# Two-layer sandwich on one core: the sums of squares of all four tiles by one selection product, and a new order of all calls

## The reference

```python
def attn(x, Wq1, Wq2, Wk1, Wk2, Wv, Wo, norm_w):
    q = silu(x @ Wq1 @ Wq2)
    f = sigmoid(x @ Wk1 @ Wk2)
    v = x @ Wv
    a = exp(log_sigmoid(f))
    k = 1.0 - a
    h = scan(h = a * h + k * v)                      # along the tokens
    out = q * h
    out = out * rsqrt(mean(out * out, axis=-1) + 1e-6) * norm_w
    return out @ Wo

def ffn(x, W1, B1, W2, B2, G, Bt):
    for i in range(6):
        x = gelu(x @ W1[i].T + B1[i]) @ W2[i].T + B2[i] + x
        if i < 5:
            x = layernorm(x) * G[i] + Bt[i]
    return x

x = x + layernorm(attn(layernorm(x), ...))
x = x + layernorm(ffn(layernorm(x), ...))
```

## Time and profile before

| | us |
|---|---|
| median of 3 runs | 627.94 (627.71 to 628.29) |
| the profiled execution, its own time | 629.86 |
| its span, first to last instruction | 628.0 |
| TensorE busy | 619.8 (99%) |
| VectorE busy | 470.1 (75%) |
| ScalarE busy | 407.9 (65%) |
| GpSimd busy | 250.4 (40%) |
| TensorE's granted clock over the span | 0.998 |

### The profile page before, as it was taken

How to read it: one execution, slowest core, us unless ns; L and a number is a source line. 1 busy time by engine, 2 the same in 40 slices (tenths; PEclk the granted TensorE clock), 3 DMA queues, 4 the chain that set the end, 5 groups by cost and what they waited for, 6 DMA issues and landing times.

```text
span 628.0 us, 8878 instructions
## 1 busy us (share of the span) xinstructions
PE 619.8 (99%) x2893; PEld 516.4 (82%) x2893; DVE 470.1 (75%) x820; ACT 407.9 (65%) x688; POOL 250.4 (40%) x232
## 2 busy tenths in 40 slices
...
GB/s 285 62 47 0 1 2 0 4 17 88 38 38 40 10 64 6 5 36 38 42 33 5 40 39 2 72 7 4 37 40 38 36 5 6 5 4 76 119 106 103
DMA packets 56877, 25.13 MB, mean 40 GB/s; under 512 B 47360, under 2 KB 52864, under 8 KB 56832
## 3 DMA queue, kind: packets, MB, share of 16 engines
...
...
## 4 chain that ended last, share of the span: by engine, by line
PE 92%; DVE 3%; issue 2%; ACT 2%; POOL 1%; POOLq 0%; DVEq 0%; ACTq 0%
PE BK L169 47%; PE BK L351 38%; PE BK L301 3%; PE BK L175 1%; PE BK L366 1%; PE BK L198 1%; DVE OL L534 1%; PE BK L242 0%; POOL X L1188 0%; ACT R L835 0%; PE BK L262 0%; PE BK L253 0%; PE BK L254 0%; PE BK L232 0%; ACT R L849 0%
## 5 line engine op out<-in xcount | busy, mean ns | idle before, releaser
L945 ACT ACTIVATE HH<-BK,B 128x512 fp32r<-128x512 f32 x192 | 132.1, 688 | 140.5 <-PE BK L169 136.2
L563 DVE TENSOR_TENSOR HL<-BK,HH 128x512 fp32r<-128x512 f32 x192 | 130.7, 683 | 83.3 <-ACT BK L951 82.8
L169 PE MATMUL BK<-XH,WL 128*128 128x512 f32 x416 | 162.5, 391 | 0.7 <-DVE HL L563 0.7
L169 PE MATMUL BK<-XL,WH 128*128 128x512 f32 x416 | 162.1, 390 | 0.0
L169 PE MATMUL BK<-XH,WH 128*128 128x512 f32 x416 | 162.0, 389 | 0.0
L351 PE MATMUL BK<-HH,WL 128*128 128x512 f32 x368 | 143.7, 390 | 0.0
L351 PE MATMUL BK<-HH,WH 128*128 128x512 f32 x368 | 143.2, 389 | 0.0
L351 PE MATMUL BK<-HL,WH 128*128 128x512 f32 x368 | 143.2, 389 | 0.0
L951 ACT ACTIVATE BK<-BK,B 128x512 f32<-128x512 f32 x192 | 125.8, 655 | 0.0
L169 PEld LDWEIGHTS BK<-XH,WL 128*128 128x128 f32 x416 | 78.1, 188 | 17.3 <-DVE HL L563 1.1
L169 PEld LDWEIGHTS BK<-XH,WH 128*128 128x128 f32 x416 | 78.1, 188 | 16.5
(11 more groups left out here) (149 smaller groups left out, 793.8 us busy)
## 6 DMA issues: line engine op xcount, KB each, us to landing
...
G<-sums SPq DMA_DIRECT2D x160, 8.0 KB, 1.8
...
sums<-P SPq DMA_DIRECT2D x40, 8.0 KB, 1.4
...
```

What stands on the lines that cost most here:

```text
L169: r = eng.matmul(dst, s, m, start=i == 0, stop=i == len(todo) - 1)
L563: eng.tensor_tensor(HL[:, g % HR, :], bank["mm1", n, j][:, :], HH[:, g % HR, :].bitcast(f32), ALU.subtract).then_inc(S["hlo"], 1)
L945: eng.activation(HH[:, g % HR, :], bank["mm1", n, j][:, :], ACT.Gelu, bias=B1[:, 8 * (n // 4) + j:8 * (n // 4) + j + 1]).then_inc(S["ghi"], 1)
```

## The change

It takes away the path with the vector of ones for tiles 0 and 1: all four tiles now run `sq_turn`, `sq_part`, one selection matmul and four `ms`. `sel()` moves from the middle of VectorE's list to its start, ahead of `ulo(0, 0)`. The written-out lists of all engines are in a new order: TensorE's up to `mm2(3, 4)`, VectorE's up to tile n = 5 and from n = 21 on, ScalarE's up to n = 4 and from n = 22 on, GpSimd's up to n = 1 and from n = 20 on, and SyncE's after its loop. No other call is added or taken away, and the loops are as before. The diff, cut:

```diff
             def rms(t, b):
                 claim(b)
-                if t < 2:
-                    pe.wait_ge(S["ssum"], 3 * t + 3)
-                    pe.wait_ge(S["one"], 1)
-                    for c in range(4):
-                        r = eng.matmul(BK[b][:, c:c + 1], SB[:, 0, c * 128:(c + 1) * 128], ONE[:, :],
-                                       start=(c == 0), stop=True, skip_group_check=True)
-                else:
-                    pe.wait_ge(S["sq_part"], t - 1)
-                    pe.wait_ge(S["sel"], 1)
-                    r = eng.matmul(BK[b][:, 0:16], SEL[:, :], PR[:, :], start=True, stop=True)
+                pe.wait_ge(S["sq_part"], t + 1)
+                pe.wait_ge(S["sel"], 1)
+                r = eng.matmul(BK[b][:, 0:16], SEL[:, :], PR[:, :], start=True, stop=True)
                 r.then_inc(S["rms"], 1)
...
-            zq(0, 2, 0); zk(0, 0, 1); v(0, 0, 2); zk(0, 1, 3); v(0, 1, 4); zk(0, 2, 5); zq(0, 3, 1); v(0, 2, 0)
-            zk(0, 3, 3); v(0, 3, 2); proj(0, 0); turn1(1, 0, 5); turn1(1, 1, 3); proj(0, 1); up(1, 0, 1); up(1, 1, 4)
-            u(1, 0); u(1, 1); proj(0, 2); zq(1, 0, 0); zq(1, 1, 5); zk(1, 0, 3); v(1, 0, 1); zq(1, 2, 2); zq(1, 3, 4)
-            rms(0, 0); zk(1, 1, 3); proj(0, 3); v(1, 1, 5); zk(1, 2, 2); v(1, 2, 3); zk(1, 3, 4); turn1(2, 0, 0)
+            zq(0, 2, 0); zk(0, 0, 1); v(0, 0, 2); zk(0, 1, 3); v(0, 1, 4); zk(0, 2, 5); v(0, 2, 0); zk(0, 3, 3)
+            zq(0, 3, 1); v(0, 3, 2); turn1(1, 0, 5); proj(0, 0); turn1(1, 1, 3); proj(0, 1); up(1, 0, 1); u(1, 0)
+            up(1, 1, 4); u(1, 1); proj(0, 2); zq(1, 0, 0); zq(1, 1, 5); zk(1, 0, 3); v(1, 0, 1); zq(1, 2, 2)
+            zq(1, 3, 4); zk(1, 1, 3); proj(0, 3); v(1, 1, 5); zk(1, 2, 2); rms(0, 0); v(1, 2, 3); turn1(2, 0, 0)
+            turn1(2, 1, 1); zk(1, 3, 4); v(1, 3, 2); up(2, 0, 0); u(2, 0); up(2, 1, 5); u(2, 1); proj(1, 0)
...
-            mm1(1, 6, 3); proj(3, 3); mm2(1, 3); rms(3, 2); mm1(1, 7, 0); mm2(1, 4); mm2(1, 5); mm2(1, 6)
-            mm1(2, 0, 1); mm2(1, 7); mm1(2, 1, 2); mm1(2, 2, 3); mm2(2, 0); mm1(2, 3, 0); turn3(3, 0, 1)
-            turn3(3, 1, 2); mm2(2, 1); mm1(2, 4, 3); mm2(2, 2); mm1(2, 5, 1); mm2(2, 3); mm1(2, 6, 2); mm2(2, 4)
-            mm1(2, 7, 0); mm1(3, 0, 3); mm2(2, 5); mm1(3, 1, 1); mm2(2, 6); mm1(3, 2, 2); mm2(2, 7); mm1(3, 3, 0)
-            mm2(3, 0); mm1(3, 4, 3); mm2(3, 1); mm1(3, 5, 1); mm2(3, 2); mm1(3, 6, 2); mm2(3, 3); mm1(3, 7, 0)
+            turn3(2, 1, 0); mm1(1, 6, 3); proj(3, 2); proj(3, 3); mm1(1, 7, 0); rms(3, 2); mm2(1, 4); mm2(1, 5)
+            mm1(2, 0, 1); mm1(2, 1, 2); mm2(1, 6); mm1(2, 2, 3); mm1(2, 3, 0); mm2(1, 7); mm2(2, 0); mm2(2, 1)
+            turn3(3, 0, 1); turn3(3, 1, 2); mm2(2, 2); mm1(2, 4, 3); mm1(2, 5, 1); mm1(2, 6, 2); mm2(2, 3); mm2(2, 4)
+            mm1(2, 7, 0); mm1(3, 0, 3); mm1(3, 1, 1); mm2(2, 5); mm2(2, 6); mm2(2, 7); mm1(3, 2, 2); mm2(3, 0)
+            mm1(3, 3, 0); mm1(3, 4, 3); mm1(3, 5, 1); mm2(3, 1); mm2(3, 2); mm1(3, 6, 2); mm2(3, 3); mm1(3, 7, 0)
...
-            def ms(t, h=None):
+            def ms(t, h):
                 ve.wait_ge(S["rms"], t + 1)
-                if h is None:
-                    eng.tensor_scalar(MS[:, t, :], bank["rms", t][:, 0:4], *to_ms(t)).then_inc(S["ms"], 1)
-                    return
...
             def sq_part(t):
-                ve.wait_ge(S["sq_turn"], t - 1)
-                if t > 2:
+                ve.wait_ge(S["sq_turn"], t + 1)
+                if t:
                     ve.wait_ge(S["rms"], t)
...
-            f_nm(3); wq1_lo(); first_xlo(0); first_xlo(1); wk1_lo(); ulo(0, 0); ulo(0, 1); q(0, 0); q(0, 1); q(0, 2)
+            f_nm(3); wq1_lo(); first_xlo(0); first_xlo(1); wk1_lo(); sel(); ulo(0, 0); ulo(0, 1); l1_st(1, 0)
...
-            ulo(1, 0); o(0, 3); ulo(1, 1); l1_st(2, 2); olo(0, 3); q(1, 0); l1_st(2, 3); q(1, 1); l1_mv(2, 0)
-            l1_mv(2, 1); l1_mv(2, 2); l1_mv(2, 3); l1_st(3, 0); l1_st(3, 1); l1_st(3, 2); l1_st(3, 3); kv(1, 0)
-            q(1, 2); q(1, 3); ms(0); scan(1, 0); l2_st(0, 0); l2_st(0, 1); l2_st(0, 2); o(1, 0); l2_st(0, 3)
+            xlo1(1, 1); l1_st(2, 2); kv(0, 3); olo(0, 2); scan(0, 3); ulo(1, 0); o(0, 3); ulo(1, 1); l1_mv(2, 2)
+            l1_st(2, 3); l1_st(3, 0); l1_st(3, 1); l1_st(3, 2); l1_mv(2, 3); olo(0, 3); q(1, 0); kv(1, 0); q(1, 1)
+            scan(1, 0); q(1, 2); o(1, 0); sq_turn(0); l2_st(0, 0); sq_part(0); l2_mv(0, 0); l2_st(0, 1); l2_st(0, 2)
+            l2_st(0, 3); ms(0, 0); ms(0, 1); l2_mv(0, 1); ms(0, 2); ms(0, 3); l2_mv(0, 2); l2_mv(0, 3); kv(1, 1)
+            q(1, 3); scan(1, 1); xlo1(2, 0); xlo1(2, 1); o(1, 1); l3_st(0, 0); kv(1, 2); l3_st(0, 1); olo(1, 0)
...
+            hlo(2, 0); hlo(2, 1); y(1, 0); hlo(2, 2); tr2(0); red2(0); hlo(2, 3); y(1, 1); xlo3(3, 0); xlo3(3, 1)
+            tr1(1); tot2(0); vae(0); red1(1); hlo(2, 4); rsb(0); hlo(2, 5); hlo(2, 6); hlo(2, 7); nn(0, 0); tot1(1)
+            mub(1); ctr(1, 0); hlo(3, 0); y(2, 0); nn(0, 1); ctr(1, 1); hlo(3, 1); y(2, 1); hlo(3, 2); tr2(1); red2(1)
+            hlo(3, 3); xlo(0, 0); tr1(2); xlo(0, 1); hlo(3, 4); red1(2); hlo(3, 5); hlo(3, 6); tot2(1); hlo(3, 7)
```

ScalarE's and GpSimd's new lists around the same place:

```diff
+            l2_nm(3, 1); ghi(2, 0); gf(2, 0); l2_nm(3, 2); l2_nm(3, 3); ghi(2, 1); sqr(0, 0); ghi(2, 2); gf(2, 1)
+            gf(2, 2); l3_nm(3, 0); sqr(0, 1); l3_nm(3, 1); l3_nm(3, 2); l3_nm(3, 3); ghi(2, 3); gf(2, 3); xn(3, 0)
+            xn(3, 1); xhi3(3, 0); xhi3(3, 1); ghi(2, 4); gf(2, 4); ghi(2, 5); ghi(2, 6); wp_hi(5); gf(2, 5); gf(2, 6)
+            ghi(2, 7); wp_hi(6); ghi(3, 0); gf(2, 7); gf(3, 0); sqr(1, 0); ghi(3, 1); wp_hi(7); ghi(3, 2); gf(3, 1)
+            sqr(1, 1); wp_hi(8); ghi(3, 3); gf(3, 2); ghi(3, 4); xhi(0, 0); gf(3, 3); xhi(0, 1); ghi(3, 5); gf(3, 4)
...
-            sum1(0); l3_ve(2); l3_ng(2); l3_rs(2); l3_nb(2); ssum(3, 2); ssum(3, 3); sum2(0); l2_ve(3); l2_ng(3)
-            l2_rs(3); l2_nb(3); x1(3, 0); x1(3, 1); x1(3, 2); x1(3, 3); l3_ng(3); l3_ve(3); l3_rs(3); wp_lo(5, 0)
-            l3_nb(3); wp_lo(5, 1); rsd(0); sum1(1); wp_lo(6, 0); wp_lo(6, 1); wp_lo(7, 0); wp_lo(7, 1); wp_lo(8, 0)
-            sum2(1); wp_lo(8, 1)
+            x1(3, 0); x1(3, 1); x1(3, 2); x1(3, 3); l3_ve(3); l3_ng(3); l3_rs(3); l3_nb(3); sum2(0); sum1(1); rsd(0)
+            wp_lo(5, 0); wp_lo(5, 1); wp_lo(6, 0); wp_lo(6, 1); wp_lo(7, 0); wp_lo(7, 1); wp_lo(8, 0); wp_lo(8, 1)
+            sum2(1)
...
```

More of the change, by code:

```diff
@@ L721, in _ @@
-            sq_part(3); ctr(0, 1); hlo(1, 5); l2_st(3, 0); l2_st(3, 1); l2_st(3, 2); l2_st(3, 3); ms(3, 0); ms(3, 1)
-            ms(3, 2); ms(3, 3); l2_mv(3, 0); l2_mv(3, 1); l2_mv(3, 2); tr2(0); l2_mv(3, 3); hlo(1, 6); red2(0)
-            hlo(1, 7); l3_st(3, 0); l3_mv(3, 0); l3_st(3, 1); l3_mv(3, 1); l3_st(3, 2); l3_mv(3, 2); l3_st(3, 3)
-            l3_mv(3, 3); hlo(2, 0); y(1, 0); tot2(0); y(1, 1); vae(0); hlo(2, 1); hlo(2, 2); rsb(0); xlo3(3, 0)
-            nn(0, 0); xlo3(3, 1); hlo(2, 3); tr1(1); nn(0, 1); red1(1); hlo(2, 4); xlo(0, 0); xlo(0, 1); hlo(2, 5)
```

204 lines of the change are left out of this document (99 added, 105 removed).

## The result

| kernel | median, us | runs | ratio to before, 95% interval |
|---|---|---|---|
| before | 627.88 (627.71 to 628.29) | 4 | 1 |
| after | 643.28 (642.82 to 644.37) | 4 | 1.0247 (1.0229 to 1.0264) |

A forecast was written before the change was run, and what follows sets the result against it. The prediction took TensorE, busy for 619.8 of 628.0 us, to set the end. Its terms, from -1.3 for the instructions to +2.2 for the largest stall, summed to +1.2 on 627.94, so 629.1 us, range 625.9 to 631.6.

The forecast's parts named there:

- 46 to 118: From 46 to 118 us: the same calls in slightly other places, VectorE idle for a fifth; 0 (0 to +1.0).
- The main step: 150 to 170 us: `put1(1)` held behind `ldp(7)`, so TensorE waits about 2 us behind `hlo(3, 0)`.
- The start: Up to `zq(0, 0)`: first products come earlier, `sel` takes part of that back; -0.2 us (-0.4 to +0.3).
- 20 to 33: 20 to 33 us: GpSimd's later squares may spare `olo(0, 2)`, its `l1_nb(1)` calls delay `wo_lo`; -0.3 us (-1.0 to +0.3).
- 33 to 46: 33 to 46 us: full VectorE delays `q(1, 3)`, stalling TensorE before `zk(1, 3)`; +1.0 us (0 to +2.0).
- 118 to 150: 118 to 150 us: less waiting at tile 3's `proj`, -0.3; `turn3(3, 0)` earlier as `wp_lo(5, 0)` moved, -0.7 us.
- 150 to 170: 150 to 170 us: a 23.6 us chain to `mm2(3, 0)` against TensorE's 21.3; stall +2.2 us (0 to +3.2).
- Behind it: After `hlo(3, 0)`: 10.5 us of calls up to `hlo(3, 3)` against 9.5 of matmuls; +1.0 us (0 to +1.5).
- The end: Kernel's end: the wait at 595 us stays, `z_ct(3, 0)` stands one call earlier; -0.2 us.
- B: Tile 1's chain, 150 to 170 us and behind, ends under its cover, both stalls fall away: 625.9 us, chance 0.24.
- D: Whole kernel: the new order changes nothing that reaches TensorE, only the instructions count: 626.6 us, chance 0.10.
- C: VectorE becomes the bound from 33 to 46 us, stall before `zk(1, 3)` 3.0 us: 631.1 us, chance 0.18.

The follow-up runs named there:

- the kernel with the swapped banks: The kernel before with only the last tile's banks swapped, `mm1(23, j)` in bank (j+1)%2: 0.9983 of before.
- the one with TensorE kept busy: The changed kernel plus 15 products with overwritten results ahead of `mm2(3, 0)`'s wait for `hlo(3, 0)`: 1.0181 of before.
- the run with the old squares: The kernel with the new order up to about 140 us and the old behind, tiles 0 and 1's squares summed the old way: 1.0014 of before.

## Why the prediction was wrong, step by step

Four steps failed. The step from 46 to 118 us was put at nothing and cost 2.2 us. The count of what stands in series stopped at tile 1, and tile 3's stall near 220 us (4.8 with its slow matmuls) lay behind it. No term of the sum is for TensorE's clock, which took 2.6 us behind `mm2(3, 0)` and 1.4 of the 4.8. And the chain to `mm2(3, 0)` was sized too short, 23.6 for 26.6 us. The main step's mechanism was right: `put1(1)` was issued 0.40 us behind `ldp(7)`, at 164.54 us, and TensorE waited for `hlo(3, 0)`.

**What bounds the kernel**: right. In the profiled executions TensorE stands or runs slowly for 15.3 us more, its own instructions take 1.0 less, and the spans differ by 14.5.

**The instructions**, -1.3: measured -1.0.

**The start**, -0.2: wrong sign. By the losses it is +0.6. `zq(0, 0)` came at 12.51 us against 12.26 in before, but that one had a late clock (last section): in the kernel with the swapped banks, whose start is that of before, it came at 11.47, and in all eight traces with the new start between 12.44 and 12.64. I followed `sel` and `first_xhi(1)`, and not `wq2_hi`, which the latter was moved past. `sel` costs little: in the old start with it ahead `zq(0, 0)` came at 11.65 and 12.18, in two executions in which the first transposes started at 6.56 and 7.09 us, and without it at 11.47 and 12.26 where they started at 6.41 and 7.12.

**20 to 33**, -0.3: measured -0.8, inside its bounds.

**33 to 46**, +1.0: measured +1.3, the right mechanism, with about half of it at the place that I named (0.67 us from start to start before `zk(1, 3)`, behind `q(1, 3)`, 0.50 of them without a record). My lists were careless: there are three `v` in TensorE's stretch, not two (the 11.8 us count three), and four `q` and six `mv` in VectorE's. Its length from the end of `ulo(1, 0)` to the end of `q(1, 3)` was 13.1 us, against 12.9. **46 to 118**, 0: measured +2.2, nearly all before 75 us. This step failed. I took VectorE's idle fifth as cover, but it is an average over 72 us; from 46 to 60 VectorE was busy for 13.42 of 14 us before the change too. What the squares push back there is not made up before tile 1's own 1.9 us come.

**118 to 150**: `proj(3)` -0.3, measured -0.5. `turn3(3, 0)` -0.7, measured -1.0; in after `l3_nb(3)` is done at 147.72 and `turn3(3, 0)` follows its neighbour.

**150 to 170**, +2.2: the chain was right, its size was not, and I missed who stands in it. From `l3_nm(3, 0)` (147.75) to `mm2(3, 0)` (174.37) it took 26.6 us, not 23.6. `put1(1)` to landing behind the load took 3.9 us from the load's issue (4.0 predicted), `rsd(0)` 2.9, the steps from `tot1(1)` to the end of `hlo(3, 0)` 2.3 (2.2). The 3.0 us too few are `got2(0)`, whose last part landed after 3.65 us instead of 1.8 (+1.9), `got1(1)` (3.9 instead of 3.1) and handovers (0.3). Some 1.4 of the 1.9 are chance, as said above: issued between the loads `ldp(5)` and `ldp(6)`, that part took 2.0 to 2.4 us in the other kernels, and in the one with TensorE kept busy the chain to the end of `hlo(3, 0)` took 24.5 us. Of the 5.2 us of standing, 1.7 come before `mm2(2, 4)`: `hlo(2, 4)` stands behind `tot2(0)` on VectorE, which waits for `got2(0)`. The prediction named what was queued behind the put and not what was queued behind this wait.

**Behind it**, +1.0 before `mm2(3, 3)`: measured 0. `hlo(3, 3)` was 2.4 us ahead of its product, since TensorE was itself late; with TensorE kept busy it was done 0.06 us ahead. (The terms of that step add up to 10.6 us, not 10.5.) Instead 2.6 us went into 13 matmuls at 427 instead of 227 ns, a cost that the prediction has no term for.

**200 to 226**, not in the prediction at all: +4.8. Stalls of 0.5 and 2.4 us and 1.4 us of slow clock. My count of the chain stopped at tile 1. That tile 3's `red1` had changed sides with tile 2's `tot2` stood in the new list, and is the same kind of step as the one that I did follow.

**The end**, -0.2: measured +0.4. The wait at 595 us stayed, as said.

**Sum.** -1.0 + 0.6 - 0.8 + 1.3 + 2.2 - 0.5 - 1.0 + 1.9 + 6.5 + 4.8 + 0.4 = +14.4, against a difference of the spans of 14.5.

**The rivals.** B and D fell: the chain didn't end under its cover. C's mechanism, a full VectorE, is real and cost 3.6 us from 33 to 75, not far from its price of 3.0, but over a longer stretch; the run with the old squares shows it. None had the large terms. A range made of cases that each have one late transfer couldn't hold a time with three stalls behind late transfers and a fallen clock behind two of them.
